# Conv, attention and experts on one core: the second half of the batch follows the first more closely

## What is computed

```python
# block 1: convolution with split attention
a = silu(conv1x1(group_norm(x, 32), w0, b0))
a = silu(conv3x3(group_norm(a, 16), w1, b1, groups=4))      # 64 -> 128 channels
y = group_norm(a, 2)                                        # seen in 8x8 windows, radix 2
g = silu(conv1x1(max_over_radix(mean_over_window(y)), w2, b2, groups=2))
g = softmax_over_radix(conv1x1(group_norm(g, 8), w3, b3, groups=2))
x = x + group_norm(einsum(y, g, weight), 32)
# block 2: causal attention; the batch is the sequence, each pixel a row of its own
h = layernorm(t);  e = tanh(h @ fc_w.T + fc_b) @ score_w
t = t + causal_softmax_average(h, e)                        # online softmax over the 16 images
# block 3: eight experts, all used, weighted per pixel by a softmax over their mean over the batch
z = layernorm(t);  w = softmax(mean_over_batch(z) @ Wr + br)
h1 = relu(bn1(z @ W1 + b1));  h2 = relu(bn2(h1 @ W2 + b2))
t = t + sum_e w[e] * (h2[e] @ Wo[e] + bo[e])
```

## Time and profile before

| | us |
|---|---|
| median of 3 runs | 169.86 |
| all runs | 169.8, 169.86, 172.09 |
| the profiled execution | 172.28 |
| its span, first to last instruction | 170.5 |
| PE busy in the span | 153.3 |
| DVE busy | 97.3 |
| ACT busy | 77.3 |
| POOL busy | 31.9 |
| mean granted TensorE clock | 0.94 |

### The profile page before, as it was taken

One profiled execution on the slowest core, in us unless ns is written; L12 is line 12 of the kernel. 1 busy time (PEld: TensorE's weight loads), 2 busy tenths in 40 slices (PEclk: granted clock), 3 DMA queues, 4 the chain that ended last, 5 costly groups with the idle time before them and its releaser, 6 DMA issues.

```text
span 170.5 us, 2730 instructions
## 1 busy us (share of the span) xinstructions
PE 153.3 (90%) x1013; PEld 69.6 (41%) x1017; DVE 97.3 (57%) x374; ACT 77.3 (45%) x131; POOL 31.9 (19%) x27
## 2 busy tenths in 40 slices
PE   6668899995898798899789899999999999999992
PEld 2222343651332364548245335355685432222420
DVE  0684895785768657189964305923102395696341
ACT  0005110505900426751159994798653796258020
POOL 7036202003210256030830600021300000000000
PEclk9987999999579999959999997899995999999999
DMA  5940000000000000000000000000000000200204
...
DMA packets 3677, 4.39 MB, mean 26 GB/s; under 512 B 193, under 2 KB 3393, under 8 KB 3537
## 3 DMA queue, kind: packets, MB, share of 16 engines
...
...
## 4 chain that ended last, share of the span: by engine, by line
PE 68%; DVE 18%; ACT 5%; POOL 3%; DMA 2%; issue 2%; ACTq 0%
PE bank L790 10%; PE bank L924 10%; PE bank L911 10%; PE bank L937 9%; PE bank L755 5%; PE bank L873 3%; DMA xin<-x 2%; PE bank L936 2%; PE bank L807 2%; PE bank L882 2%; PE bank L832 2%; DVE y L605 2%; PE bank L840 2%; PE bank L735 2%; DVE ctxs L667 2%
## 5 line engine op out<-in xcount | busy, mean ns | idle before, releaser
L397 ACT ACTIVATE h<-bank,s_bnb,s_bns 128x512 f32<-128x512 f32 x32 | 23.2, 780 | 8.5 <-PE bank L911 5.0
L755 PE MATMUL bank<-warm 128*128 128x512 bf16 x76 | 23.1, 442 | 1.7 <-ACT y L334 1.5
L911 PE MATMUL bank<-xs,par 64*128 64x512 f32 x64 | 18.9, 668 | 0.6 <-ACT h L397 0.5
L924 PE MATMUL bank<-h,f2s 64*64 64x512 f32 x128 | 19.1, 670 | 0.0
L790 PE MATMUL bank<-pad,w 32*64 32x512 f32 x288 | 17.4, 593 | 0.2 <-DVE pad L501 0.2
L755 PEld LDWEIGHTS bank<-warm 128*128 128x128 bf16 x80 | 8.2, 112 | 11.7 <-issue 6.0
L334 ACT ACTIVATE y<-bank,par 128x512 f32<-128x512 f32 x8 | 4.8, 688 | 16.0 <-PE bank L790 16.0
L748 PE MATMUL bank<-warm 128*128 128x512 bf16 x32 | 9.8, 461 | 1.3 <-POOL warm L301 1.3
L790 PEld LDWEIGHTS bank<-pad,w 32*64 32x64 f32 x288 | 7.7, 130 | 7.6 <-issue 5.9
L543 DVE BATCH_NORM_STATS2 s_ws<-y 128x6 f32<-128x64 f32 x64 | 8.8, 209 | 1.2 <-ACT y L334 1.0
L911 PEld LDWEIGHTS bank<-xs,par 64*128 64x128 f32 x64 | 4.9, 187 | 7.8 <-issue 4.1
...
## 6 DMA issues: line engine op xcount, KB each, us to landing
...
```

The lines of the kernel that those rows point to most:

```text
L397: A.activation(h1[(2 * m + h) % 4][:], bank[Z1[h]][:], ACT.Relu, bias=tile("bnb", P, 3 * EP)[:, col:col + 1], scale=tile("bns", P, 3 * EP) ...
L755: T.matmul(bank[Z1[0]][:], warm[:, 0:P], warm[:], start=True, stop=True)
L911: ins = T.matmul(bank[Z1[h]][:], f1[own, e, :], xs[own, k, q], start=True, stop=True)
L924: ins = T.matmul(bank[Z2[h]][at:at + C, :], f2s[rows, h, e, :], h1[(2 * m + h) % 4][rows, :], start=True, stop=True)
```

## The change

The list is written anew, with `xr` as a new step and 34 matmuls in `heat` steps instead of 80. Layer 1 is cut to four matmuls of 64x64. Two additions on DVE sum the four pairs of an `xs` tile before `logits`, which then has 4 matmuls instead of 16. `t2` turns the context by four transposes of 128x128 instead of eight products of 128x64. The bias products of both k go together, once for each q, as two matmuls on 32 rows each; for that the turned router weights and the bias rows are laid out twice, 32 partitions apart, with zeros between.

```diff
 ORDER = [(s.split(".")[0], int(s.split(".")[1])) for s in """
-    warm.0 warm.1 silu0.0 warm.2 warm.3 warm.4 silu0.1 warm.5 gn1.0 warm.6 gn1f.0 silu.0 warm.7 warm.8 silu.1 warm.9 gn1.1 xnorm.0 warm.10
-    bn.0 gn1f.1 warm.11 warm.12 gn2.0 warm.13 silu.2 warm.14 warm.15 gn2f.0 silu.3 xnorm.1 conv.0 conv.1 silu.4 norm0.0 conv.2 bnf.0
-    conv.3 conv.4 gn2.1 conv.5 gn2f.1 conv.6 conv.7 conv.8 silu.5 norm0.1 ws.0 ws.1 ws.2 ws.3 s2row.0 conv.9 conv.10 conv.11 conv.12
-    silu.6 conv.13 conv.14 gn3.0 gn3f.0 win.0 conv.15 conv.16 conv.17 silu.7 ws.4 w2.0 ws.5 heat.0 ynorm.0 heat.1 gna.0 heat.2 heat.3
-    ynorm.1 gnaf.0 heat.4 ws.6 heat.5 w3.0 ws.7 heat.6 wan.0 heat.7 gate.0 heat.8 outp.0 heat.9 gate.1 heat.10 heat.11 heat.12 gn4.0
-    gn4f.0 heat.13 heat.14 gn3.1 heat.15 x1.0 gn3f.1 heat.16 ln1.0 heat.17 ln1.1 heat.18 tok.0 heat.19 heat.20 heat.21 heat.22 heat.23
-    win.1 ynorm.2 heat.24 hn.0 heat.25 w2.1 heat.26 hch.0 heat.27 hn.1 hch.1 fc.0 fc.1 heat.28 score.0 gna.1 heat.29 coef.0 heat.30 gnaf.1
-    att.0 heat.31 heat.32 wan.1 heat.33 cen.0 scan.0 gate.2 ynorm.3 w3.1 ln2.0 gate.3 cen.1 heat.34 ln2.1 outp.1 heat.35 gn4.1 xn2.0
-    heat.36 xt.0 heat.37 heat.38 gn4f.1 heat.39 xn2.1 x1.1 l1.0 xt.1 ln1.2 ln1.3 tok.1 l1.1 l2.0 l1.2 l2.1 hch.2 hn.2 hn.3 hch.3 l1.3 fc.2
-    fc.3 l2.2 score.1 coef.1 l1.4 l2.3 cen.2 l1.5 l2.4 att.1 scan.1 ln2.2 l1.6 xn2.2 l2.5 cen.3 l1.7 ln2.3 xt.2 l2.6 xn2.3 l1.8 t2.0 t2.1
-    l2.7 xt.3 l1.9 logits.0 l2.8 t2.2 wt.0 l1.10 wb.0 l2.9 l1.11 wb.1 l2.10 l1.12 mix.0 mix.1 l2.11 l1.13 mix.2 mix.3 mix.4 mix.5 mix.6
-    mix.7 l1.14 l2.12 mix.8 mix.9 mix.10 mix.11 mix.12 finish.0 mix.13 l2.13 mix.14 mix.15 l1.15 l2.14 mix.16 mix.17 mix.18 mix.19 t2.3
-    mix.20 mix.21 mix.22 mix.23 l2.15 mix.24 mix.25 mix.26 mix.27 mix.28 finish.1 mix.29 mix.30 mix.31 finish.2 finish.3
+    silu0.0 warm.0 silu0.1 gn1.0 silu.0 warm.1 warm.2 gn1f.0 warm.3 warm.4 xnorm.0 warm.5 warm.6 gn1.1 silu.1 warm.7 bn.0 warm.8 gn2.0
+    gn1f.1 warm.9 warm.10 warm.11 warm.12 bnf.0 warm.13 warm.14 gn2f.0 xnorm.1 conv.0 conv.1 conv.2 silu.2 norm0.0 silu.3 silu.4 conv.3
+    conv.4 gn2.1 conv.5 gn2f.1 conv.6 norm0.1 ws.0 conv.7 ws.1 ws.2 conv.8 ws.3 silu.5 s2row.0 warm.15 conv.9 conv.10 conv.11 conv.12
+    conv.13 conv.14 gn3.0 silu.6 gn3f.0 win.0 conv.15 conv.16 ws.4 conv.17 ws.5 w2.0 silu.7 gna.0 heat.0 heat.1 ws.6 gnaf.0 ws.7 heat.2
+    wan.0 gate.0 gate.1 heat.3 ynorm.0 heat.4 ynorm.1 w3.0 heat.5 heat.6 heat.7 outp.0 gn4.0 heat.8 gn3.1 gn4f.0 gn3f.1 x1.0 win.1 heat.9
+    ln1.0 ln1.1 heat.10 hn.0 ynorm.2 heat.11 tok.0 heat.12 w2.1 heat.13 heat.14 heat.15 hn.1 heat.16 hch.0 hch.1 fc.0 fc.1 score.0 gna.1
+    coef.0 gnaf.1 att.0 ynorm.3 wan.1 cen.0 cen.1 w3.1 scan.0 gate.2 ln2.0 gate.3 ln2.1 outp.1 xt.0 l1.0 xn2.0 gn4.1 xt.1 xn2.1 gn4f.1
+    x1.1 l1.1 l2.0 ln1.2 ln1.3 tok.1 hn.2 l1.2 l2.1 l1.3 l2.2 xr.0 hn.3 hch.2 l1.4 hch.3 xr.1 fc.2 l2.3 fc.3 l1.5 coef.1 score.1 l2.4
+    cen.2 att.1 l1.6 l2.5 scan.1 cen.3 ln2.2 ln2.3 l1.7 xn2.2 l2.6 xt.2 l2.7 xn2.3 l1.8 t2.0 xt.3 xr.2 t2.1 l1.9 xr.3 l2.8 logits.0 l1.10
+    l2.9 wt.0 t2.2 wb.0 l1.11 l2.10 wb.1 l1.12 l2.11 mix.0 mix.1 l2.12 l1.13 mix.2 mix.3 mix.4 mix.5 mix.6 mix.7 mix.8 mix.9 l2.13 l1.14
+    mix.10 mix.11 mix.12 mix.13 mix.14 mix.15 l1.15 l2.14 t2.3 mix.16 mix.17 l2.15 mix.18 mix.19 mix.20 mix.21 mix.22 mix.23 mix.24 mix.25
+    finish.0 mix.26 mix.27 mix.28 finish.1 mix.29 mix.30 finish.2 mix.31 finish.3
 """.split()]
...
-            sp.dma_start(row_par[:], row_params).then_inc(rows_loaded, 16)
+            sp.dma_start(row_par[0:STRIP], row_params).then_inc(rows_loaded, 16)
+            sp.dma_start(row_par[STRIP:2 * STRIP], row_params).then_inc(rows_loaded, 16)
...
+            def sum_pairs(n):
+
+                dve.wait_ge(xs_ready, n + 1)
+                x, two = xs[:, n // Q, n % Q], tile(f"xtwo{n}", P, 2, P)
+                V.tensor_tensor(two, x[:, 0:2, :], x[:, 2:4, :], ALU.add).then_inc(pairs_added, 1)
+                dve.wait_ge(pairs_added, n + 1)
+                V.tensor_tensor(tile(f"xsum{n // Q}{n % Q}", P, P), two[:, 0, :], two[:, 1, :], ALU.add).then_inc(xsum_ready, 1)
...
                 for i in range(PK):
-                    for h in range(2):
-                        T.matmul(bank[OUT[k][q]][h * C:(h + 1) * C, i * P:(i + 1) * P], ctxs[:, k, q, 2 * i + h, :], w("ident"),
-                                 start=(i == 0), stop=False)
+                    pe.wait_ge(ctx_ready, context_at(k, q, 2 * i + 1))
+                    T.matmul(bank[OUT[k][q]][:, i * P:(i + 1) * P], pair_of(ctxs, k, q, i), w("ident"), is_transpose=True,
+                             start=(i == 0), stop=False)
...
-                        pe.wait_ge(xs_ready, max(Q + 1, k * Q + q + 1))
-                        for i in range(PK):
-                            ins = T.matmul(bank[SMALL][:, q * E:(q + 1) * E], xs[:, k, q, i, :], w("wr"),
-                                           start=(k == i == 0), stop=(k == NK - 1 and i == PK - 1))
+                        pe.wait_ge(xsum_ready, max(Q + 1, k * Q + q + 1))
+                        ins = T.matmul(bank[SMALL][:, q * E:(q + 1) * E], tile(f"xsum{k}{q}", P, P), w("wr"),
+                                       start=(k == 0), stop=(k == NK - 1))
...
-                    ins = T.matmul(bank[Z1[h]][:], f1[own, e, :], xs[own, k, q], start=True, stop=True)
+                    for j in range(2):
+                        to = slice(j * C, (j + 1) * C)
+                        ins = T.matmul(bank[Z1[h]][to, :], f1[own, e, to], xs[own, k, q], start=True, stop=True)
...
-                if m % PER_OUT == 0:
-                    pe.wait_ge(rows_loaded, 16)
+                if m % (NK * PER_OUT) == 0:
+                    pe.wait_ge(rows_loaded, 32)
                     pe.wait_ge(small_free, SMALL_AT["wt", 0])
-                    turned = tile("wT", Q * E, P).rearrange("p (o n) -> p o n", o=1).broadcast_to([Q * E, PK, P])
-                    for half in range(2):
-                        at = q * P + half * C
-                        T.matmul(bank[OUT[k][q]][half * C:(half + 1) * C, :], r_("bo")[:, at:at + C], turned, start=False, stop=False)
+                    for s in range(NK):
+                        turned = tile("wT", NK * STRIP, P)[s * STRIP:(s + 1) * STRIP].rearrange("p (o n) -> p o n", o=1).broadcast_to([STRIP, PK, P])
+                        T.matmul(bank[OUT[s][q]][:], r_("bo", s)[:, q * P:(q + 1) * P], turned, start=False, stop=False)
```

More of the change, by code:

```diff
@@ L42 @@
 Q = 2
+STRIP = 32
 EPS = 1e-5
@@ L100, in w, with r_ @@
             return par[0:rows, a:b]
-        row_par = sb("row_par", [Q * E, n_rows])
-        def r_(name):
+        row_par = sb("row_par", [NK * STRIP, n_rows])
+        def r_(name, strip=0):
             a, b = row_where[name]
-            return row_par[:, a:b]
+            return row_par[strip * STRIP:(strip + 1) * STRIP, a:b]
         xin = sb("xin", [P, PAIRS, PIX])
@@ L527, in fold_weights @@
                 V.memset(tile("lowest", P, BK), LOWEST)
+                V.memset(tile("wsoft", P, NK * STRIP), 0.0)
                 V.memset(runmax[:, :, 0], LOWEST)
@@ L682, in routing_weights @@
                 step(V.reciprocal(sm, sm))
-                V.tensor_tensor(tile("wsoft", P, Q, E), ex, each(sm, P, Q, E), ALU.mult).then_inc(wt_ready, 1)
+                soft = tile("wsoft", P, NK * STRIP)
+                for s in range(NK):
+                    V.tensor_tensor(soft[:, s * STRIP:s * STRIP + Q * E].rearrange("p (q e) -> p q e", q=Q), ex,
+                                    each(sm, P, Q, E), ALU.mult).then_inc(wt_ready, 1)
             def weights_turned():
                 dve.wait_ge(small_ready, SMALL_AT["wt", 0])
-                V.tensor_copy(tile("wT", Q * E, P), bank[SMALL][0:Q * E, 0:P]).then_inc(small_free, 1)
+                V.tensor_copy(tile("wT", NK * STRIP, P), bank[SMALL][0:NK * STRIP, 0:P]).then_inc(small_free, 1)
             def weigh(m):
@@ L887, in weights_transposed @@
                 small(("wt", 0))
-                pe.wait_ge(wt_ready, 1)
-                T.transpose(bank[SMALL][0:Q * E, 0:P], tile("wsoft", P, Q * E), w("ident")).then_inc(small_ready, 1)
+                pe.wait_ge(wt_ready, NK)
+                T.transpose(bank[SMALL][0:NK * STRIP, 0:P], tile("wsoft", P, NK * STRIP), w("ident")).then_inc(small_ready, 1)
             def weights_spread(q):
                 small(("wb", q))
-                pe.wait_ge(rows_loaded, 16)
+                pe.wait_ge(rows_loaded, 32)
                 for e in range(EP):
                     at = (q * EP + e) * P
-                    ins = T.matmul(bank[SMALL][:, e * P:(e + 1) * P], r_("sel")[:, at:at + P], tile("wT", Q * E, P), start=True, stop=True)
+                    ins = T.matmul(bank[SMALL][:, e * P:(e + 1) * P], r_("sel")[:, at:at + P], tile("wT", NK * STRIP, P)[0:STRIP], start=True, stop=True)
                 ins.then_inc(small_ready, 1)
@@ L1048, in lay_out @@
         lo, hi = row_where[name]
-        rows_par[:, lo:hi] = a
```

(1 more changed line is left out.)

18 lines of the change are left out of this document (11 added, 7 removed).

## The result

The changed kernel takes 165.56 us (median of 4 runs, 164.69 to 166.65), the kernel before in the same comparison 170.98. The ratio is 0.970, 95% interval 0.965 to 0.975. 165.4 us was forecast. The profiled execution took 164.99 us with a span of 163.2, against 170.5.

A forecast was written before the change was run, and what follows sets the result against it. The prediction took the chain before `tok.1` as bound by latency and DVE's queue order, the dense stage by PE, the clock as second limit. Its terms summed to -4.45 us; against the median 169.86 that gave 165.4 us, range 161 to 170.

The forecast's parts named there:

- Ahead of the convolution: Before `conv.0`: `bnf` ahead of `gn2f.0` costs 2.35 us, an earlier first 1x1 product gains 0.45; +1.9 us (1.35 to 2.35).
- (a): Chain up to `w3.0`: `ws.5` ahead of `w2`'s half, and ten filler matmuls ahead of `w3.0`; +0.9 us (0.2 to 1.3).
- (b): Chain: `gn3.1` now stands ahead of `gn4f.0`, no longer in the shadow of POOL's power; +0.55 us (0.5 to 0.7).
- (c): End of the chain: `gn4.1`'s statistics wait behind `xn2.0`, which waits for the power of `ln2.0`; +1.5 us (1.4 to 1.6).
- (d): Chain: removing 46 filler matmuls gives nothing, as the chain waits for other engines; +0, upper bound +1.5 us.
- router's sums: Dense stage, `logits`: four matmuls remain, taking about 1.0 us instead of 3.74; -2.7 us.
- context transposed: Dense stage, `t2`: four transposes of about 0.5 us in place of each step's products; -1.7 us (-1.2 to -2.0).
- joint bias: Dense stage: two bias pairs instead of four groups of 1.00 us; -2.0 us, or -0.3 if strips run one after the other.
- layer 1 and its neighbours: Dense stage: faster layer 1 (-0.6) and neighbouring `l1` and `l2` of one shape (-1.3); -1.9 us (0 to -2.5).
- The clock: Dense stage: low-clock spell behind `logits` gone, the one behind `score.1` likely stays at less cost; -2.4 us (0 to -3.2).
- rival 5: From the 1x1 convolution to `tok.1` and in the dense stage: low-clock spells make it slower than before, 171.0 us; chance 0.09.
- What comes back: Dense stage: new PE waits for ACT's ReLUs, the scan and the power of `ln2.3`; +4.1 us (2 to 5.5).

The follow-up runs named there:

- The second run: The changed kernel with `bnf` back behind `norm0.0`: median 164.98 us (161.93 to 166.44), no ratio given.
- the last run: The old order with the new arithmetic, with `gn1.1` moved behind `xnorm.0`: median 161.97 us, ratio 0.950 to the kernel before.
- the eighth run: The order of the kernel before with all 80 heat matmuls and the new arithmetic, `t2.3` moved ahead of `mix.16`: 161.95 us, ratio 0.946 to the kernel before.
- the third run: The changed kernel with `gn4.1` ahead of `xn2.0` again and `l1.1`, `l2.0` behind `tok.1`: median 166.34 us, ratio 0.974 to the kernel before.
- the second one: Profile of the changed kernel run again without an edit: 166.55 us, ratio 0.973 to the kernel before, span 164.9.
- the fifth run: The changed kernel with the router's sums back on TensorE as 16 matmuls, without DVE's additions: 169.02 us, ratio 0.984 to the kernel before.

## Why the prediction was right, step by step

**Ahead of the convolution**, +1.9, measured +2.24, inside its bounds. The second run puts 2.0 of it on `bnf` alone. The gain from `xnorm.0` ahead of `gn1.1` did not show, since the filler in front of it ran at the low clock as feared (eight matmuls in 3.57 us); the last run shows that even at the full clock only 0.3 us of it reaches `conv.0`.

**The chain**, moves (a) and (b). (a) was said at +0.9 and came to +0.2 at `w3.0` and to -0.16 at `outp.0`: the spell there lasted 3.4 us, not 6.6 as in the earlier trace rows, so ten filler matmuls took 3.7 us, not 4.5, and `w3.0` itself ran at the full clock. Against the eighth run, whose spell is as short, the new list costs 0.5 here. (b) gave +0.5, as said. (c) gave +1.5 between `coef.0` and `gn4.1`, as said, 1.4 of it shown by the third run, which also shows that it is a fair trade. The 4.85 came to 3.94 since (a) was over-counted and 0.36 us came back ahead of `coef.0`, where a filler step is gone between `fc` and `score.0`. (d), the removal of filler, was priced at +0 up to 1.5 us. That row of the sum held in the first profile, where no spell fell on path work; in the second a spell on `fc` and `score.0`, which more filler might have kept away, cost 1.45 us. The bound was right for the 46 that went. Its reason, that the chain waits for other engines, is too simple: the run without any filler puts 6 to 7 us on it, and in the old order a spell of 3.4 us in the chain cost 1.57.

**PE's work.** Four terms, each with a run of its own:

| term | said | from the timelines | by taking it back |
|---|---|---|---|
| router's sums | -2.7 | -2.75 | -2.7, and -1.5 of clock |
| context transposed | -1.7 | -1.6 | -1.7 |
| joint bias | -2.0 | -1.9 | -2.2 |
| layer 1 and its neighbours | -1.9 | -0.2 per pair | -1.6 |

**The clock**, -2.4 said. In the first profile both spells of the dense stage are gone, -3.2; in the second one is left at the place named. The chance given to the other side (rival 5) rested on a true mechanism, but in the dense stage 2.4 us of new waits, in pieces of at most 1.3 us, brought no spell, and the 24 narrow records that went took one away, as the fifth run shows. In the chain idle time does bring the low clock: in the run without filler PE was busy for 9.0 of 20.3 us and stayed at 1.2 GHz throughout.

**What comes back**, +4.1 said, +2.4 measured (3.15 less 0.79). The wait behind `tok.1` was sized at 1.5 and took 1.0, the wait for the scan at 1.3 and took 0.5, the one around `xt.2` at 1.9 and took 1.7. The places were right. The scan's was the worst of the sizes, and ACT's part was over-counted too: all waits of PE for ReLUs in the stage sum to 1.3 us. I added the durations of the earlier trace rows, 2.7 us for the ReLUs of one `l1` and `l2`, but neighbouring records on ACT overlap by 0.1 us. From start to start a full round takes 2.48 us in the profile after:

```profile
99.84 1.45 ACT L399 ACTIVATE h<-bank,s_bnb,s_bns 128x512 f32<-128x512 f32 x2
101.19 1.26 ACT L407 ACTIVATE y<-bank,s_bnb 128x512 f32<-128x512 f32 x2
102.32 0.61 ACT L371 ACTIVATE xnorm<-bank 128x512 f32<-128x512 f32 x1
```

That explains part of the 1.7 us; the rest I have not taken apart. The `mix` term of -0.6 has no run of its own and stays argued.

**The sum.** -4.45 said, -7.3 in the first profile, -5.4 between the medians. The difference between the two is the clock again: the profile before lies 1.3 us above its median, the one after 0.6 below its own. So 165.4 against 165.56 is closer than the steps deserve. Lateness was said 0.9 us too high, waits 1.7 too high, and the clock's gain 0.8 too low. Between the medians the forecast difference was 1.0 us too small, and the base of 169.86 turned out 1.1 us below the median of the comparison; that these two cancel is luck.

**What the prediction did not say**, although its terms had it: the order and the arithmetic pull in opposite directions. The lateness of 4.85 and the waits of 4.1 stood in the sum beside -2.1 and parts of -1.9 and -0.6, all from the order alone. Their sum was positive. The eighth run shows it: with the old order the same arithmetic takes 161.95 us. Most of the loss is one step of the list, `bnf`: 2.0 us.
